# Moving the scaling of the gated output and the level-64 product in a software-pipelined gated delta rule

## The reference, cut to what matters

```python
def step(S, inp):
    qt, kt, vt, gt, bt = inp
    S = S * jnp.exp(gt)[:, None, None]
    kv = jnp.einsum('hk,hkv->hv', kt, S)
    delta = (vt - kv) * bt[:, None]
    S = S + kt[:, :, None] * delta[:, None, :]
    o = jnp.einsum('hk,hkv->hv', qt, S)
    return (S, o)
...
gated = core * jax.nn.silu(z)
gated = gated * jax.lax.rsqrt(jnp.mean(gated * gated, axis=-1, keepdims=True) + EPS)
gated = gated * norm_w
return gated.reshape(B, Tn, VDIM) @ W_out
```

## Time and profile before

| what | value |
|---|---|
| median of 3 runs | 3361.2 us (3358.42 to 3363.03) |
| the profiled execution | 3358.48 us, span 3356.8 us |
| mean granted TensorE clock | 0.979 of 2.4 GHz |
| the recurrence, from the first to the last line 524 | 392 to 3000 us |
| matmuls of line 524 in it | 1024, eight in each of 128 slots |

### The profile page before, as it was taken

The page is one execution under the profiler, slowest core; times in us unless marked ns, Lnnn a source line. Parts: engine busy times, 40 slices in busy tenths (PEclk is TensorE's granted clock), DMA queues, the critical chain, the costliest instruction groups (busy, mean ns, idle before and its releaser), DMA issues. The chain is left out here.

```text
span 3356.8 us, 69394 instructions
## 1 busy us (share of the span) xinstructions
PE 3136.6 (93%) x22505; PEld 2207.7 (66%) x22505; DVE 2347.3 (70%) x4805; ACT 1820.3 (54%) x5914; POOL 1669.2 (50%) x3745
## 2 busy tenths in 40 slices
PE   6997699999999999999999999999999999988998
PEld 4555477667667666676677666767676766765565
DVE  3433577777777777777777777777777777754776
ACT  4222466666666666665666666656665666532332
POOL 1001566666656666665666666656666666620000
PEclk9998899999999999999999999999999999997999
DMA  3000111111111111111111111111111111101000
GB/s 73 1 1 19 40 37 40 38 37 38 41 35 41 34 41 35 40 35 41 34 41 34 42 34 41 35 41 35 44 39 38 39 44 35 34 13 38 7 7 13
DMA packets 447073, 113.89 MB, mean 34 GB/s; under 512 B 350497, under 2 KB 445841, under 8 KB 446673
## 3 DMA queue, kind: packets, MB, share of 16 engines
q1 hardware_dynamic: 446672, 108.98, 14.5%
HBM read 63.85 MB, written 45.09 MB: 32 GB/s over the span
## 5 line engine op out<-in xcount | busy, mean ns | idle before, releaser
L1152 DVE SCALAR_TENSOR_TENSOR conv<-raw,ckq,conv 128x512 f32<-128x512 f32 x384 | 342.9, 906 | 18.9 <-ACT conv L886 9.7
L466 POOL TENSOR_TENSOR Tb<-Tb,btmp 64x14 f32<-64x14 f32 (+6 forms) x896 | 290.0, 324 | 70.8 <-POOL btmp L462 1.2
L1152 DVE SCALAR_TENSOR_TENSOR conv<-raw,cv,conv 128x512 f32<-128x512 f32 x384 | 307.3, 814 | 9.1
L850 ACT ACTIVATE kd<-bank,gs 128x128 f32<-128x128 f32 x512 | 146.4, 368 | 285.4 <-PE bank L718 285.4
L462 POOL TENSOR_TENSOR btmp<-Bk,Tb 64x14 f32<-64x14 f32 (+6 forms) x896 | 249.7, 279 | 65.6
L392 POOL TENSOR_SCALAR ty<-ty 128x4 f32<-128x4 f32 x128 | 29.2, 228 | 507.8 <-issue 392.2
L926 ACT ACTIVATE gatn<-gat,ty 128x128 f32<-128x128 f32 x512 | 163.6, 390 | 203.2 <-POOL ty L441 201.5
L678 PE MATMUL bank<-xnT,wkq 128*128 128x512 f32 x512 | 259.5, 631 | 12.8 <-DMA ckq<-in_L_attn_conv_w_dram 10.3
L524 PE MATMUL bank<-S,ykq 128*128 128x256 f32 x1024 | 259.6, 397 | 12.3 <-issue 12.3
L885 ACT ACTIVATE raw<-bank 128x512 f32<-128x512 f32 x256 | 153.1, 598 | 215.2 <-PE bank L678 215.0
L1098 DVE SCALAR_TENSOR_TENSOR N<-ET,ty,bank 128x128 f32<-128x128 f32 x512 | 143.7, 343 | 177.3 <-POOL ET L408 177.2
(11 more groups left out here) (350 smaller groups left out, 7717.8 us busy)
## 6 DMA issues: line engine op xcount, KB each, us to landing
blk_n<-N SPq DMA_DIRECT2D x128, 256.0 KB, 2.5
Tp<-blk_t SPq DMA_DIRECT2D x128, 128.0 KB, 2.9
Wp<-blk_w SPq DMA_DIRECT2D x128, 128.0 KB, 2.9
wkq<-in_L_attn_W_qkvz_dram SPq DMA_DIRECT2D x32, 128.0 KB, 2.2
wv<-in_L_attn_W_qkvz_dram SPq DMA_DIRECT2D x16, 256.0 KB
Bk<-blk_n SPq DMA_DIRECT2D x64, 64.0 KB, 2.7
blk_t<-Tb SPq DMA_DIRECT2D x64, 64.0 KB, 2.5
blk_w<-Wb SPq DMA_DIRECT2D x64, 64.0 KB, 2.5
```

The source lines that it names most:

```text
L466: pool.tensor_tensor(Tb[:, j + 1:, 0:j], Tb[:, j + 1:, 0:j], tmp, ALU.subtract).then_inc(row_rdy, 1)
L850: i = act.activation(kd[t.c % RING][:, u, :], bU[2][:, u // 2], ACT.Copy, scale=gs[t.c][:, DEC, u:u + 1])
L1152: dve.scalar_tensor_tensor(out=conv[h][:, j], in0=raw[h][:, j, :, k:k + 256], scalar=cw[:, j, k:k + 1], in1=conv[h][:, j], op0=ALU.mult, o ...
```

## The change

Three moves, one on each of three engines. TensorE: `w64` goes from the end of the slot to the place behind `state_in` in the next slot, in front of `x16`; it works on the same step, so its lag is S_L + 1. ScalarE: `normed` goes from the end of the slot to the place behind `expo` in the next slot, with lag S_E instead of S_D. VectorE: `rhs` and `add_w64` change places. No instruction is added or removed.

```diff
                 def w64(s):
-                    t = s.back(S_L)
+                    t = s.back(S_L + 1)
...
                 def body(s):
                     state_in(s)
+                    w64(s)
                     x16(s)
...
                     x64(s)
                     project_out(s)
-                    w64(s)
                     norm_tp(s)
...
                 def normed(s):
 
-                    t = s.back(S_D)
+                    t = s.back(S_E)
...
                     norms(s)
                     expo(s)
+                    normed(s)
                     kdec(s)
...
                     xev64(s)
-                    normed(s)
                     norm_ev(s)
...
                 def body(s):
                     accumulate(s)
+                    rhs(s)
                     add_w64(s)
-                    rhs(s)
                     gate(s)
```

## The result

The changed kernel takes 3255.15 us (3250.84 to 3257.23, 4 runs) against 3360.03 us before: ratio 0.9685, 95% interval 0.9668 to 0.9702.

A forecast was written before the change was run, and what follows sets the result against it. TensorE, busy 93% of the span, was taken as the bound. -50 - 42 + 12 = -80 us took the profiled 3358.5 to 3278.5; with 2.7 us for the median, 3281 us, range 3262 to 3315.

The forecast's parts named there:

- part two: TensorE: the level-64 product (line 620) moved beside line 542 saves 0.33 us a slot, 42 us over 128 slots.
- The borders: TensorE, the 128-wide side of a tile-size change: 0.11 us coming out of 64-wide work, 0.09 going in.
- the 0.13 inside the group: TensorE, line 620's eight matmuls: worth 0.47 us but taking 0.60, so 0.13 for a group's start and end.
- the steady pace: TensorE, inside a 64-wide group: tiles follow each other 0.058 us apart, the ground for taking 42 us.
- Part one: ScalarE's scaling moved behind the exponential removes line 644's wait for zz in odd slots: 50 us, bounds 36 and 61.
- give-back: TensorE's line 542 in odd slots waits for the reload of Tp from DRAM: 12 us lost, bounds 0 and 13.
- Costs taken as 0: ScalarE's moved instructions fit in kdec's 2.30 us wait; VectorE's copy behind the right-hand side delays nothing: both 0.
- Rival B: Only the scaling's gain comes through, as the reload of Tp sets the odd slots: 3311 to 3323 us; chance 0.12.
- C: Another wait replaces zz in odd slots, so only the level-64 product's move counts: 3331 us; chance 0.05.
- D: Slower: the reload comes later against TensorE, long enough for the clock to fall; up to 3430 us; chance 0.03.
- E: No effect: TensorE's waits only move to the next reload or copy; 3361 us; chance 0.02.
- 61 us for part one: Upper bound at line 644, 1.02 us x 60 waits; with 42 and a reload keeping up, 3258 us; chance 0.03.

The follow-up runs named there:

- e4: The changed kernel with line 542 behind the transposes of line 633, so lines 620 and 542 are no longer side by side; 3284.1 us, ratio 0.978.
- e5: The changed kernel with the matmuls of lines 620 and 542 issued in one group, unit by unit; 3305.2 us.
- e2: The kernel before with only the TensorE and VectorE moves, the scaling staying at the end of ScalarE's slot; 3321.4 us, ratio 0.9895.
- e3: The changed kernel with VectorE's old order, the level-64 copy ahead of the right-hand side; 3368.0 us, ratio 1.0024 to the kernel before.
- e10: The changed kernel with lines 620 and 542 as one group and inverse rows 6 and 7 done early by GpSimd; 3192.8 us, ratio 0.9512.
- e1: The kernel before with only ScalarE's scaling moved, TensorE and VectorE in their old order; 3324.8 us, ratio 0.9898.
- e9: The changed kernel with inverse rows 6 and 7 done by GpSimd in the odd slot instead of the even one; 3225.6 us, ratio 0.9611.
- e8: The kernel before with the scaling moved and line 542 alone put behind lines 633 and 638; 3331.4 us.
- e11: The kernel before with the scaling moved and inverse rows 6 and 7 done early by GpSimd; 3290.5 us, ratio 0.9797.
- e12: The kernel before with only inverse rows 6 and 7 done early by GpSimd; 3287.6 us, ratio 0.9788.

## Why the prediction was wrong

The step that failed is the size in part two, "With lines 620 and 542 side by side one excursion goes: 0.11 + 0.09 + 0.13 = 0.33 us in a slot. Times 128 slots: 42 us." It is 0.51, 65 us; the 23 us between are nearly all of the 25 that the forecast missed by. The borders were read rightly: 0.10 at line 747 (1.93 to 1.83), 0.11 within line 524 (1.93 to 1.82). The term that failed is the third, the 0.13 inside the group: together the two lines take 0.90 us, where they took 0.60 and 0.61, so it is 0.31. What I did not see is that two small groups do not follow each other but overlap. I let line 542's 0.60 follow line 620's 0.47, and took the steady pace for the limit of the array. That they overlap is shown by the trace of the change, by e4 (apart: the 0.51 are gone) and by e5 (mixed: 0.62 for both). The earlier trace rows had the hint: line 620's eight matmuls and line 542's sixteen both take 0.6 us, since line 542 uses two tiles at once and line 620 leaves three of four idle. The Trainium skill (TensorEngine Tiling (Array Packing), Key Properties) says in the line below the one I cited that different tiles can load weights and multiply in parallel; the trace agrees, with line 542 0.29 us behind line 620.

- Part one, 50 us: the mechanism is right, the wait at line 644 is gone and nothing takes its place on ScalarE. Alone it brought 33, on top of part two 66 (e2 to the change). What can be said without the neighbour: waits at lines 644 and 542 cost 68.7 together.
- The give-back, 12 us: right in place (line 542, odd slots, the reload). Part one and give-back came to 38 in my sum; measured, 68.7 - 29.5 = 39.2. Each by itself was too small, and they made up for each other by luck: the 68.7 hold line 542's old waits, which I had left standing, and the give-back is more than twice the 12.
- Costs taken as 0: kdec kept 1.14 us of its wait. The swap on VectorE was costed at nothing with the copy behind the right-hand side, which held for the wait at line 644; but with the later copy the silu came onto line 392 (0.23 to 0.33 us on average), which I had not looked for, and e3 shows how much hangs on that order: 113 us.
- Line 542 waits more often and longer, as forecast (26 times for 21, longest 3.8 us for 2.2), but its idle time in all is not more (15.9 us for 16.9); the cost shows in the length of the odd slots.
- Rival B (part one alone) and C (part two alone) fall, as both are in the trace. D, the clock: 0.98 as before. E falls.

The range missed because its low end took 61 us for part one as the only way to a larger gain. No bound of part two lay above 42, though no row showed two small groups side by side.

## What to carry to other kernels

Where small matmuls run alone on a part of the array, put those of another product that uses other tiles beside them, issued as one group: it saves the change of tile size and the time itself. The group waits for the later of its inputs, though: here it lost 50 us (e5) until the reload was out of the way, and gained 33 behind that (e10). When a wait is taken away on the engine that bounds, look for the next input of that engine in the same slot and follow it back through every queue, since the reload here took back 30 us, and new orders on TensorE and VectorE moved it too. Moving work to where a third engine has slack (two rows on GpSimd) was worth 30 us in the change, 72 in the kernel before and 112 in e5, with no change on the busy engine.

## What the runs showed that I had not expected

- Matmuls on three 64 x 64 tiles at once: 24 in the time of 16 (e5, 0.62 us for both lines, even slots 19.34 to 19.06 us).
- GpSimd's short instruction of 0.23 us, where it met VectorE's two-operand instruction of 1.21 us, ended 0.1 us behind it: it took 0.33, 0.61, 0.89 and 0.93 us on average in the change, e5, e3 and e4. The order on VectorE so sets the time of a chain that is not seen to wait for VectorE.
- A store of 64 KB to DRAM followed by its reload takes 2.54 us from issue to issue in most pairs and 3.5 to 4.7 in some, 13 of 64 in e1, 10 in e9 and none in e4 and e8. The cause was not tried.
- The last slot of each pass of the loop is about 2 us longer than its neighbours in the kernel before, in the change and in e11 and e12; nothing here tells why.
